# Six of seven attentions rebuilt: split-operand projections over three groups, score units in pairs, no filler matmuls

## What is computed

```
h = tokens(x)
h = LN(h + neighbour_attention(h))         # attention 1: heads of 16, a 3x3 kernel over the scores
h = LN(h + (causal attention; then 8 experts of 768, top 2, with a capacity))   # attention 2, ffn 0
h = LN(h + (attention without the diagonal + projection + residual))            # attention 3
4 T5 layers: h += attention(rms(h)) Wo     # heads of 64, with relative bias: attentions 4 to 7
             h += relu(rms(h) wi) wo       # ffn 1 to 4; in layers 1 and 3 also 8 experts, top 2
h = LN(h + ...)
# one attention, per head:
q, k, v = nx @ Wq, nx @ Wk, nx @ Wv ; p = softmax(q @ k.T + mask or bias) ; y = p @ v ; h += y @ Wo
```

## Time and profile before

| | |
|---|---|
| three runs | 2470.09, 2473.28, 2479.43 us, median 2473.28 |
| profiled execution | 2461.45 us, its span 2459.6 us |
| TensorE, weight loads | busy 91%, 82% |
| VectorE, ScalarE, GpSimd | busy 45%, 28%, 27% |
| granted TensorE clock | 0.85 of full over the span |
| chain that ended last | TensorE 70%, issue 17%, VectorE 8% |
| DMA | 146.51 MB, 60 GB/s mean |

### The profile page before, as it was taken

The page is one execution under the profiler, slowest core; times in us unless marked ns, Lnnn a source line. Parts: engine busy times, 40 slices in busy tenths (PEclk is TensorE's granted clock), DMA queues, the critical chain, the costliest instruction groups (busy, mean ns, idle before and its releaser), DMA issues.

```text
span 2459.6 us, 39394 instructions
## 1 busy us (share of the span) xinstructions
PE 2240.1 (91%) x14241; PEld 2011.7 (82%) x14241; DVE 1115.6 (45%) x3192; ACT 699.9 (28%) x1728; POOL 672.0 (27%) x2238
## 2 busy tenths in 40 slices
PE   7999999696999999999999989979999999998991
PEld 7998888595888788888888878968888888887881
DVE  2553344542454345633544634336653254463437
ACT  1232222241222123322222244413332222224430
POOL 4464122304454311251111400044316011240002
PEclk8895899697999579995866899979999586789995
DMA  4085000252000000010000256510001000015641
GB/s 115 18 284 169 14 5 12 72 171 71 8 1 1 13 1 1 1 39 1 1 8 8 62 174 202 185 57 10 1 1 39 1 1 8 8 40 188 203 149 39
DMA packets 75589, 146.51 MB, mean 60 GB/s; under 512 B 6136, under 2 KB 56514, under 8 KB 74725
## 3 DMA queue, kind: packets, MB, share of 16 engines
q1 hardware_dynamic: 69062, 131.72, 17.5%
q0 software_dynamic: 6336, 12.26, 1.7%
HBM read 103.90 MB, written 41.05 MB: 59 GB/s over the span
## 4 chain that ended last, share of the span: by engine, by line
PE 70%; issue 17%; DVE 8%; POOL 2%; ACT 1%; DMA 1%; SPq 0%; DVEq 0%; POOLq 0%; ACTq 0%
PE ps_proj L857 19%; PE ps_score L892 10%; PE ps_o L915 7%; PE ps_proj L869 6%; PE ps_score L886 5%; PE ps_proj L938 5%; PE ps_pt L903 5%; PE ps_score L1008 4%; PE ps_proj L992 3%; PE ps_proj L926 2%; DVE o L1275 1%; PE ps_score L889 1%; PE ps_proj L829 1%; DVE v L1385 1%; DVE prob L1261 1%
## 5 line engine op out<-in xcount | busy, mean ns | idle before, releaser
L857 PE MATMUL ps_proj<-xt,aw_big 96*128 96x111 f32 x2376 | 396.4, 332 | 0.0
L857 PEld LDWEIGHTS ps_proj<-xt,aw_big 96*128 96x128 f32 x2376 | 370.0, 243 | 9.3 <-issue 4.7
L1155 POOL TENSOR_TENSOR tmp<-rs 111x1 f32<-111x1 f32 x462 | 101.0, 219 | 978.4 <-DVE rs L1232 953.9
L892 PEld LDWEIGHTS ps_score<-kt,qt 64*111 64x111 f32 (+1 forms) x1848 | 235.3, 198 | 101.7 <-issue 74.7
L892 PE MATMUL ps_score<-kt,qt 64*111 64x111 f32 (+1 forms) x1848 | 294.7, 300 | 24.7 <-DVE logit L1452 12.4
L1008 PE MATMUL ps_score<-w,hid 128*112 128x192 f32 (+2 forms) x1680 | 303.6, 333 | 5.9 <-DVE x L1535 5.9
L1008 PEld LDWEIGHTS ps_score<-w,hid 128*112 128x112 f32 (+2 forms) x1680 | 276.0, 179 | 7.8 <-DVE x L1535 7.4
L915 PEld LDWEIGHTS ps_o<-v,probt 111*111 111x111 f32 x1848 | 242.9, 204 | 9.5 <-issue 2.6
L915 PE MATMUL ps_o<-v,probt 111*111 111x65 f32 (+1 forms) x1848 | 247.1, 272 | 2.3 <-ACT probt L1080 2.1
L1080 ACT ACTIVATE probt<-ps_pt 111x333 f32<-111x333 f32 x308 | 136.8, 444 | 313.2 <-PE ps_pt L903 313.2
L1099 ACT ACTIVATE hid<-ps_proj 128x224 f32<-128x224 f32 (+2 forms) x360 | 137.0, 383 | 251.8 <-PE ps_proj L992 251.6
(11 more groups left out here) (196 smaller groups left out, 3785.1 us busy)
## 6 DMA issues: line engine op xcount, KB each, us to landing
w_in<-w_all_dram SPq DMA_DIRECT2D x50, 768.0 KB, 4.5
w<-w_all_dram SPq DMA_DIRECT2D x50, 576.0 KB, 4.8
rows_in<-w_lo SPq DMA_DIRECT2D x1, 12320.0 KB, 58.8
rows_out<-w_lo SPq DMA_DIRECT2D x1, 9240.0 KB, 85.2
tin<-rows_in SPq DMA_DIRECT2D x36, 224.0 KB
aw_big<-aw_t_dram SPq DMA_DIRECT2D x4, 1728.0 KB, 10.4
rows_out<-tout SPq DMA_DIRECT2D x36, 168.0 KB
patch<-patches_dram SPq DMA_DIRECT2D x11, 333.0 KB, 3.3
```

The lines of the kernel that those rows point to most:

```text
L857: last = pe.matmul(bank[:, i * TG:(i + 1) * TG], w, src, start=(n == 0), stop=(n == len(terms) - 1))
L892: last = pe.matmul(bank[0:TG, i * TG:(i + 1) * TG], qt[p:p + s.rows, par, c, :], kt[p:p + s.rows, par, c, :], start=not s.pe_mask, stop=Tr ...
```

## The change

- The six attentions after the first use the split operands of the feed-forward stages: A splits (ScalarE and VectorE) into `xa_hi`, `xa_lo`, `xb`, and a step QK projects one piece of 128 outputs for a block of three groups (the last block has two) in five fp32r matmuls; V is five matmuls for each half of 384 columns (T5), or for all 192.
- Their weights are maps in the same memory array as the feed-forward ones and come through the same W1 steps, into a ring that has now three places: two loads each for causal and diagonal, three for a T5 layer (Q, K, V). The output weights have one buffer, `wo`.
- Scores are issued for a pair of units, the passes of the two alternating; E, PT and PV are done for pairs. A round is S(n), E(n), PT(n-1) twice, PV(n-2), n counting pairs. `prob` and `probt` have four places.
- V is copied by ScalarE, the scale of the queries is applied by ScalarE. For T5 the division is done for each half as soon as it is there.
- There are no filler matmuls.
- COMB and GAT of a preceding stage are placed two to a group. GpSimd's Newton step has three operations instead of four; it copies 64 more columns after more of the norms.
- The first attention (`neigh_order`) keeps its order; it gets the steps W1 for the two weight loads of the causal attention, at n = 24 and n = 32.

```diff
+def att_fill(a, g, last_stage, follower):
+    if last_stage in COMBINED and g < G:
+        for c in (3 + 2 * g, 4 + 2 * g):
+            if c < G:
+                fill.append(("prev", ("COMB", c)))
+                if c + GAT_RING < G:
+                    fill.append(("prev", ("GAT", c + GAT_RING)))
+    if g < G:
+        b = BLOCK_OF[g]
+        i = g - BLOCKS[b][0]
+        if b + 1 < NB:
+            g0, n = BLOCKS[b + 1]
+            if i == 1:
+                fill += [("A", x) for x in range(g0 + 2, g0 + n)]
+                fill += [("QK", b + 1, j) for j in range(s.qk // 2)]
+            elif i == 2:
+                fill += [("QK", b + 1, j) for j in range(s.qk // 2, s.qk)]
+    if 2 <= g:
+        fill.insert(0, ("OT", g - 2, s.vparts - 1))
+    if g + 1 < G:
+        fill += [("V", g + 1, j) for j in range(s.vparts)]
+    if 2 <= g:
+        fill.append(("Y", g - 2))
...
+    if g < G and i == 0 and b + 1 < NB:
+        fill += [("A", x) for x in range(g0, min(g0 + 2, g0 + n))]
...
+    if a == DIAG:
+        fill += {2: [("W1", r)], 9: [("W1", r + 1)], 10: [("W1", r + 2)]}.get(g, [])
+    elif g == (2 if a == CAUSAL else 9):
+        fill.append(("W1", r))
+    if s.t5 and 1 <= g:
+        fill.append(("OT", g - 1, 0))
+def att_order(a, last_stage, follower):
+    out = first_block(a) if last_stage[0] == "ffn" else []
+    pairs = 2 * G
+    for n in range(pairs + 2):
+        g, p = divmod(n, 2)
...
+        if n < pairs:
+            steps += [("S", g, p), ("E", g, p)]
+        if 1 <= n <= pairs:
+            h, q = divmod(n - 1, 2)
+            steps += [("PT", h, 2 * q), ("PT", h, 2 * q + 1)]
+        if n >= 2:
+            steps.append(("PV", *divmod(n - 2, 2)))
+        for x in steps:
+            out.append(x)
+            if x[0] == "S":
+                continue
+            gap += 1
+            upto = min(-(-count * gap // 8), count)
+            out += fill[given:upto]
@@ neigh_order
+        if n in (24, 32):
+            out.append(("W1", LOAD0[("att", CAUSAL)] + (n == 32)))
@@ TensorE, S
-                    if a in (CAUSAL, DIAG) and (a == DIAG or g):
-                        if a == CAUSAL and g == 1 and u == 0:
-                            pe.wait_ge(w1_ready, 1)
-                        full = w1_hi[:, 1 if a == DIAG else 0, :, :].rearrange("p c n -> p (c n)")
-                        for _ in range(DENSE[u]):
-                            pe.matmul(bank, full[:, 0:128], full[:, 0:512], start=True, stop=True,
-                                      skip_group_check=True)
+                    banks = [score_bank((*key, e)) for e in range(2)]
...
+                    for i in range(3):
+                        for e, bank in enumerate(banks):
+                            c, at = s.heads(2 * p + e)[i]
+                            ins = pe.matmul(bank[0:TG, i * TG:(i + 1) * TG],
+                                            qk[at:at + s.rows, b % 2, c, t0:t0 + TG],
+                                            qk[at:at + s.rows, b % 2, s.chunks + c, t0:t0 + TG],
+                                            start=not s.pe_mask, stop=True, skip_group_check=True)
@@ TensorE, QK and V
+                    terms = [(w1_hi, 0, hi), (w1_hi, 0, lo), (w1_lo, 0, hi), (w1_hi, 1, two), (w1_lo, 1, two)]
+                    for i, (w, c, src) in enumerate(terms):
+                        last = pe.matmul(bank[:, 0:n * TP], w[:, slot, c, at:at + 128], src, start=(i == 0),
+                                         stop=(i == len(terms) - 1))
+                    terms = [(xa_hi, w1_hi, 0), (xa_hi, w1_lo, 0), (xa_lo, w1_hi, 0), (xb, w1_hi, 1), (xb, w1_lo, 1)]
@@ TensorE, PT
+                pe.wait_ge(prob_ready, n + 1)
+                if n:
+                    pe.wait_ge(pt_taken, n)
@@ ScalarE
+                    for e in range(1 if a == NEIGH else 2):
+                        if ATTS[a].t5:
+                            act.wait_ge(shifted, unit(a - T5, g, v) + 1)
+                        else:
+                            act.wait_ge(score_taken[n % 2], n // 2 + 1)
+                        act.activation(prob[:, at, :, :], prob[:, at, :, :], ACT.Exp).then_inc(prob_ready, 1)
...
                     act.wait_ge(w1_raw, 16 * (r + 1))
+                    if r >= W_RING:
+                        act.wait_ge(proj_full, LAST_PROJ[r - W_RING] + 1)
@@ GpSimd, norm
-                    link(pool.tensor_tensor(t, r, r, ALU.mult))
-                    link(pool.tensor_tensor(t, t, v, ALU.mult))
-                    link(pool.tensor_scalar(t, t, -0.5, 1.5, ALU.mult, ALU.add))
-                    link(pool.tensor_tensor(r, r, t, ALU.mult))
+                    link(pool.tensor_scalar(t, r, r, v, ALU.mult, ALU.mult))
+                    link(pool.tensor_scalar(t, t, -3.0, r, ALU.add, ALU.mult))
+                    link(pool.tensor_scalar(r, t, -0.5, None, ALU.mult))
```

More of the change, by code:

```diff
@@ L178, in att_order @@
             fill = []
[L179 to L185, removed]
-                fill.append(("TOK", g + 3))
[L187 to L192, removed]
+            if g + 3 < G:
+                fill.append(("TOK", g + 3))
+            more = qkv(NEIGH, g + 1) if g + 1 < G else []
+            fill += more
+            if g >= 3:
                 fill.append(("N2", g - 3))
@@ L195, in att_order @@
                 fill.append(("A", g + 2))
[L196 to L205, removed]
+            if g == G - 1:
+                fill += [("next", ("A", i)) for i in range(3)]
+            if g == G:
+                fill += [("next", x) for x in first_block(CAUSAL)]
             count, given, gap = len(fill), 0, 0
[L207 to L211, removed]
+        if n == 8:
+            out.append(("LATE",))
+        if n in (24, 32):
+            out.append(("W1", LOAD0[("att", CAUSAL)] + (n == 32)))
         steps = []
@@ L301, in routed_order @@
             out.append(("U", 2 + k, m))
-            if m == 1 and k < n:
-                out.append(("W1", r + k + 2))
             if m == 2 and k + 1 < n:
                 out.append(("X", k + 1))
+            if m == 2 and (k < n or not last):
+                out.append(("W1", r + k + 2))
             if k and m in (2, 5):
@@ L315, in routed_order @@
             out += [("COMB", g), ("GAT", g + 4)]
-    out += [] if last else [("next", ("A", 0))]
+        if m == 2 and not last:
+            out.append(("W1", r + n + 3))
+    out += [] if last else [("W1", r + n + 4), ("next", ("A", 0))]
     out.append(("D", 3 + n, 0))
@@ L319, in routed_order @@
     out.append(("D", 3 + n, 1))
+    out += [] if last else [("next", ("A", 2))]
     if last:
@@ L366, in numbered @@
         key = (st, *step)
-        if step[0] in ("TOK", "Q", "K", "V", "OT", "Y", "U"):
+        if step[0] in ("TOK", "Q", "K", "QK", "V", "OT", "Y", "U"):
             proj[key] = len(proj)
-            if step[0] == "U":
-                hidden[key] = len(hidden)
+        elif step[0] == "S" and st[1] != NEIGH:
+            for e in range(2):
+                score[(*key, e)] = len(score)
         elif step[0] in ("S", "L", "CNT", "D"):
@@ L547, in tower @@
         patch_in = [sem(f"patch_in{i}") for i in range(PATCH_RING)]
[L548 removed]
+        aw_in = sem("aw_in")
+        wo_in = sem("wo_in")
         w1_raw = sem("w1_raw")
@@ L888, in att_step @@
[L888 to L894 removed]
+                            proj_out((st, what, g, 0))
@@ L896, in att_step @@
                 elif kind == "PT":
-                    u = step[2]
-                    n = unit(a, g, u)
-                    pe.wait_ge(prob_ready, n + 1)
-                    if n:
-                        pe.wait_ge(pt_taken, n)
-                    for i in range(3):
-                        last = pe.transpose(ps_pt[0:TG, i * TG:(i + 1) * TG], prob[:, n % 3, i, :], ident)
-                    last.then_inc(pt_full, 1)
+                    turn_prob(NEIGH, g, step[2])
                 elif kind == "PV":
@@ L916, in att_step @@
+                    if u == 0 and g:
+                        pe.wait_ge(o_ready, g)
+                    for i, (c, p) in enumerate(ATTS[NEIGH].heads(u)):
+                        h = ATTS[NEIGH].head(c, p)
+                        at = (h % 6) * (SMALL_D + 1)
+                        last = pe.matmul(ps_o[0:TG, h // 6, at:at + SMALL_D + 1],
+                                         probt[:, unit(NEIGH, g, u) % 4, i, :], v16[:, g % 3, h, :],
                                          start=True, stop=True, skip_group_check=True)
@@ L928, in att_step @@
+                    for i, (c, n) in enumerate([(3 * j + i, 128) for i in range(3)] if s.t5 else [(0, 128), (1, 64)]):
+                        last = pe.transpose(bank[0:n, i * TG:(i + 1) * TG], o[:, g % 2, c * 128:c * 128 + n], ident)
                     last.then_inc(proj_full, 1)
```

668 lines of the change are left out of this document (385 added, 283 removed).

## The result

The changed kernel takes 2658.25 us (2655.17 to 2660.23, 4 runs) where the kernel before takes 2471.69 (2434.54 to 2479.43, 4 runs): a ratio of 1.084, interval 1.070 to 1.097. The forecast was 2630, in a range of 2440 to 2790, with slower at 0.73.

What follows compares the result with a forecast made beforehand. The prediction took TensorE's stream of work and its granted clock as the bound. From 2461.45 us, -39 (full-clock sums), +64 (late load) and +132 (clock) gave 2618, about 2630 on the median; range 2440 to 2790.

Steps and rivals of the forecast that it cites:

- The new wait: In each pair TensorE stands while ScalarE waits for VectorE's two softmaxes, bank copies queued behind; 3.5 us in the first pair.
- The late load: Causal attention's second weight load, queued behind zero-fills in the first attention: 57 us idle, causal scores at 304, +64 us.
- The fifth rival: The late load holds nobody, its bytes going past the zero-fills: 64 us less in any case; chance 0.15.
- The clock: In the attentions, gaps in TensorE's work slow the passes behind them: 0 to 3.4 us for each of 132 pairs.
- I take 1.0: The price in us chosen for slow passes behind the gap in each of 132 pairs: +132 us.
- The rival in which the clock holds (2498): The attentions' wait is exposed but gaps cost no clock: 2498 us, or 2419 with scores side by side; chance 0.23.
- half clock everywhere (3060): TensorE at half clock in all six attentions after the first: some 3060 us; chance 0.05.
- The full-clock sums: The six attentions' new times, waits included, with TensorE at full clock: together -39 us.
- rival 1: Score passes on two row sets run side by side: 0.6 us less a pair, 79 less, 2551 us; chance 0.20.
- rival 3: The attentions' wait is covered and TensorE stays the bound: 2096 us on the profile, 2108; chance 0.10.
- The extra casts and splits of the weights: Sixteen more on ScalarE and VectorE beside TensorE's work, costed at nothing; 48 us in all without that cover.

Runs made afterwards that it cites:

- Experiment 1: The changed kernel with the exponentials of a pair moved behind both transposes of the pair before: 2359.12 us, ratio 0.952 to the kernel before.
- Experiment 9: The kernel before with each unit's exponential behind its own scores, transposes still two units behind: 2474.45 us, ratio 0.989.
- experiment 6: The changed kernel with six dense passes behind the first transpose of each pair, first nine groups, inside TensorE's wait: 2587.45 us, ratio 1.057.
- Experiment 4: The changed kernel with the two units of a pair scored one after the other, passes not alternating between row sets: 2666.04 us, ratio 1.075.
- experiments 1, 3, 10: Changed kernel, exponentials behind both transposes; 3 adds the causal attention's second weight load at step 43 (2305.64 us); 10 also spreads a block's turns over groups (2281.90 us).
- experiment 8: Changed kernel with exponentials behind both transposes and second load at step 43, plus six dense passes before each causal and diagonal score pair: 2330.32 us, ratio 0.937.
- experiment 7: The kernel before with only its 504 dense filler passes taken out: 2550.66 us, ratio 1.029.

## Why the prediction was right, and where two errors met

Stretch by stretch, cut at the first projection or score and at the last output product in both traces (working: full-clock change plus 1.0 us for each of 22 pairs, as forecast):

| part | before | after | change | forecast |
|---|---|---|---|---|
| start to the causal scores | 240.3 | 305.1 | +64.8 | +64 |
| causal | 214.2 | 230.2 | +16.0 | +14 |
| ffn behind it | 142.1 | 160.5 | +18.4 | 0 |
| diagonal and first T5 | 457.0 | 519.3 | +62.3 | +53 |
| second T5 | 295.7 | 272.9 | -22.8 | -17 |
| ffn behind it | 230.3 | 237.7 | +7.4 | 0 |
| third T5 | 220.1 | 291.2 | +71.1 | +60 |
| fourth T5 | 297.6 | 273.0 | -24.6 | -17 |
| all else | 362.3 | 367.8 | +5.5 | 0 |
| span | 2459.6 | 2657.7 | +198.1 | +157 |

**The new wait: right in place and in size.** TensorE was said to stand until ScalarE has passed both exponentials; it does, released by the copy of OT. For the first pair of a block the forecast had that copy start 5.3 us behind the scores and last 0.44, with a wake-up of 0.15: 5.9. Measured in the pair above: 5.84. The T5 groups come every 22.6 to 24.3 us on the mean of a layer (forecast about 23), the causal and diagonal ones every 20.0 (forecast 19). Experiment 1 shows the cause: 299 us by the order alone. Experiment 9 corrects how it should be told: it isn't the exponential behind its own scores, but that together with two units in a step and the shorter distance to the transposes.

**The late load: right**, 54 us of idle time forecast as 57. That the start of the causal scores is met within about 1 us is luck: ScalarE resumes at 236.5 and not at 230, the rest takes 69 us and not 74, and other traces with the same first attention start at 289 to 298. The fifth rival is out.

**The clock: right in kind, the size was off.** The term that was mis-sized is "I take 1.0". In the group at 1060.6 the two pairs take 24.6 us in the changed kernel and 20.6 in experiment 6 (1022.4 to 1043.0), all of that at full clock: 2.0 us a pair, within the stated range of 0 to 3.4. Over a stretch, busy time by one less the clock gives 47 us lost in the first T5 layer (172.64 x 0.27) and about 80 in the causal and the diagonal one each (176.05 x 0.46), which is 2.1 and 3.7 a pair; an upper bound, as part of it lies beside VectorE's chain. The rival in which the clock holds (2498) is out. So is half clock everywhere (3060): that came true in the causal and the diagonal attention, but not in the T5 layers.

**The full-clock sums: too high.** They make the other half of the total come out. The clock's upper bounds of all six attentions add up to 333 us, 2.5 a pair, where the forecast put 132; so the sums at full clock can be too high by up to 200. The third group of a block was put at 21.5 and takes 20.6. Twelve score passes with the switch behind them take 0.77 a pair; at the pace that I took they would take 1.36 (0.77 for six, and six more at 0.1). That is the 0.6 of rival 1, so rival 1 was right about its mechanism. The Trainium skill (TensorE: Matmul & The Clock Gate, section "The mechanism") says that matmuls on different row groups run concurrently; by that rule, the trace agrees: 0.77 us for twelve passes as for six. The price of rival 1, 79 us, is not shown. Experiment 4 brings back 0.28 of the 0.59 us on TensorE and nothing in the chain, so that its 8 us don't measure it. In the chain the forecast had VectorE begin 1.54 us behind the first score. It begins after less than 1 us in about 28 of the 88 pairs of the T5 layers, and after more than 1.5 in about 51, where it first has other work to finish, as the output at 1061.72. So in most pairs the earlier scores can't have brought the whole 0.6: the forecast priced the pass and not the place in VectorE's queue. In the five rows of attentions the two errors cancel down to 9 us (102 measured, 93 forecast), so that 2630 is nearer to the result than its terms deserve. (One sum on record has a slip: 17.5 less 5.6, 1.3 and 0.4 is 10.2, not 10.5. It enters rival 3 alone, by some 7 us.)

**Not foreseen:** 31 us outside the attentions, 18 of them in the ffn behind the causal one. In the waits of that stretch TensorE stands 31 us for GpSimd's norms instead of 23, which is a part of it; the rest stays open. In the third T5 layer the first group takes 38.9 us (first scores at 1787.2 and 1826.1), with or without the edit of experiment 1 (1590.1 and 1629.0), where the forecast had 8 for everything that is special to that layer; TensorE waits there for GpSimd's norms (4.1 and 5.1 us) and for the transpose copy (6.0 and 3.5). The extra casts and splits of the weights, put at nothing, were not tested by themselves.

**Rival 3, TensorE as the bound (2108),** needed an order that hides the chain. With that order (experiments 1, 3, 10) the time falls to 2282, not to 2108. One part of the difference is that the causal and the diagonal attention run at 0.55 to 0.63 of the clock; the six filler passes of experiment 8 did not make that pay.

## What to carry to other kernels

Before two units share a step, count what stands in each in-order queue between the one's result and the other's release: a wait of ScalarE for VectorE costs nothing while the transposes are two units behind (+464 us of wait, no time), and 299 us when two units share the step, the transposes are one step behind and bank copies are queued after it. Count a gap of TensorE as the gap and the slow passes behind it; in the pair shown the second was as large as the first (2.45 and 2.43 us). Work taken off TensorE is not time taken off, as long as another engine sets the pace or the clock falls with it: look at busy time times clock, not at busy time. And ask what an experiment leaves as it was: changing the order of the twelve passes left the start of VectorE where it was.

## What the hardware showed that was not expected

- A TensorE that is busy for 199.65 of 200 us can be granted 0.50 of its clock (experiment 7). What the engine did in that stretch was narrow f32 passes, without the dense ones; a full busy row is no promise of full clock.
- Twelve f32 score passes alternating between two sets of 64 rows take 0.77 us; six on one set take the same 0.77, and twelve in two runs of six 1.05.
- Six useless dense passes in each pair, inside a wait of 2.4 us, made a kernel 71 us faster; eight of the same kind just behind the wait made it 114 us slower.
